# Edge stage of a graph layer: block numbers loaded one or two at a time, accumulator slots cleared by GpSimd, plain addition

## The chip, the cores and the metric

One of the cores of a Trainium2 chip runs the whole program. The metric is device time in microseconds (us) of one execution. Its engines are called as in the profile: PE (TensorE; PEld its weight loads), DVE (VectorE), ACT (ScalarE), POOL (GpSimd) and SP (SyncE); a name with q is an engine's own instruction queue (sequencer).

## What is computed

A node table x of 6250 rows by 256 goes through a layer norm, two graph attention layers plus a linear attention branch, and a mixture of eight experts. The part that matters here is one graph layer; there are two, over the same 106,250 edges, sorted by destination:

```python
q = (x @ Wq + bq).reshape(n, H, C)          # H = 4, C = 64
k = (x @ Wk + bk).reshape(n, H, C)
v = (x @ Wv + bv).reshape(n, H, C)
e = (edge_attr @ We).reshape(-1, H, C)      # edge_attr: 106250 x 194
kj = k[src] + e
vj = v[src] + e
logits = einsum('ehc,ehc->eh', q[dst], kj) / sqrt(C)
ex = exp(logits - segment_max(logits, dst)[dst])
a = ex / (segment_sum(ex, dst)[dst] + 1e-16)
out = segment_sum(vj * a[:, :, None], dst).reshape(n, H * C) + x @ Ws + bs
```

## The kernel before

The nodes form 49 blocks of 128 (NB), the sorted edges tiles of 128. A tile whose edges reach over a block's border is visited once per block, so the work is a list of 880 **slots** (NS), each a pair of a tile and a block. `plan` makes that list on the device: `g.tab` holds, for each slot, the tile's number and, from z.NSP on, the block's number, and `g.flag` is 1 where a slot has the same block as the one before it and 0 where a new block begins.

`nodes` makes the projections of each layer. Keys and values go to memory (`kvD`); the queries of block b stay in SBUF, in the first 256 columns of slot b + 1 of `g.acc`, whose slots have A = 260 columns (four heads of 64 and a denominator each). The edge stage adds up its result in the same array: the sum of block b goes to slot b, which is free once the queries of block b - 1 have been used for the last time. Block b's own queries lie one slot further. The addition L969 has to overwrite the old content at the first slot of a block and to add at the others, so it multiplies what is there by the flag: `acc = acc * flag + pa`.

`edges` (from L745) runs 44 **chunks** of T = 20 slots. Four are written out, then a loop runs 20 times with two chunks a turn (`chunks`, L796), then two more follow in which only late work is left. VectorE, which does a pair of slots at a time (q = 0 to 9 in a chunk), has this order per pair:

- `add` (L964 to L970) of the first slot of a pair that is LAG = 36 slots back;
- L1016, kj: keys plus the edge product; L1028, vj: values plus the edge product;
- `add` of the second slot;
- L1041, the product of kj and the queries; L977, `reduce`, of the pair before.

At fixed q it also does the running maxima over a block: at q = 2 the scans L1061 and L1062 and the copy L1063, at q = 3 the transpose L998, the scans L1024 and L1025 and L1034 to L1036, at q = 4 L1044 and L1056, at q = 5 L1019, L1020 and L1031, at q = 8 the rescaling L1007; at q = 0 and 5 it makes a one-hot matrix (L961, 128 x 1280).

TensorE does, for each slot: two matmuls of the edge attributes (L916; each is two passes in the trace), the queries of the slot's block spread to its edges (L919, two passes) and, for the slot 36 back, the segment sum pa (L938, two passes), which waits for the addition two slots before it. ScalarE makes the weighted values w (L897, L899) and the matrices `oht` (L872, L874). GpSimd issues the gathers of keys and values, one per slot (L859); `kv` is a ring of ten slots, so the two gathers of a pair wait until vj of the pair five earlier is done (L857). SyncE loads the edge attributes, also by a table of numbers.

A block's number picks an address, so it must be in a register of the engine that uses it. `table` (L100) loads a row of numbers from `g.tab` into registers; in the trace this is a TENSOR_LOAD of line L102 in the engine's queue, with the queue's register steps (FUSED_REGOPS, ALU_OP) around it. TensorE loads ten numbers ahead of slots 0 and 10 of a chunk (L912). VectorE loads ten at q = 3 (L1000), ahead of the addition, ten or four at q = 8 (L1002), and six at the head of the loop (L995).

The order of the instructions on each engine is the order of the code; the engines wait for one another by semaphores (`wait_ge`, `need`).

## Time and profile before

| | us |
|---|---|
| median of three runs | 5624.68 |
| lowest and highest run | 5619.65, 5625.87 |
| the profiled execution's own time | 5591.4 |
| its span, first to last instruction | 5589.5 |
| PE busy | 4402.2 |
| DVE busy | 4000.3 |
| ACT busy | 2763.5 |
| POOL busy | 2149.0 |

The two edge stages lie at about 474 to 2403 and 2643 to 4594 us of the span. In the profile a group of instructions is given with its line, engine and operation, what it writes and reads, its count, its busy time and the mean of one, and then the idle time of its engine just before such instructions and what ended it. The releaser "issue" means that the engine waited for nothing that the profile shows, as when its queue is still at work on the instruction.

### The profile page before, as it was taken

To read this page: it belongs to the slowest core of one execution; us is meant where nothing else is said; L and a number is where in the kernel's file an instruction comes from. 1 tells how busy PE (TensorE), PEld (TensorE's weight loads), DVE (VectorE), ACT (ScalarE), POOL (GpSimd) and SP (SyncE) were. 2 spreads that over 40 slices of the span, in tenths; PEclk is the share of its full clock that TensorE was granted. 3 is DMA by queue.
4 is the path that set the end of the run, shared out by engine and by line. 5 is a ranking of instruction groups with operands and counts; after the bars stand their busy time and mean duration, and the time that the engine had idled before them with its cause. 6 is when DMAs were issued, how large, how long until landed. Compare 5 with 4: busy or idle time off the path is not lost. (4 is left out here: it accounts for less than half of the span.)

```text
span 5589.5 us, 99514 instructions
## 1 busy us (share of the span) xinstructions
PE 4402.2 (79%) x18414; PEld 3403.3 (61%) x18415; DVE 4000.3 (72%) x8475; ACT 2763.5 (49%) x10075; POOL 2149.0 (38%) x2298
## 2 busy tenths in 40 slices
PE   3977988888888888878988888888888873139980
PEld 1546777777777777633777777777777752126650
DVE  4446988888888888854988888888888877302222
ACT  0122666666666666631566666666666661013320
POOL 1013544444444444300544444444444424430005
PEclk9999999999999999989999999999999985569995
DMA  4468666666666666534866666666666633432225
GB/s 94 135 217 243 187 182 187 185 181 186 182 191 189 180 187 182 150 112 148 235 185 185 182 181 188 182 183 183 179 186 180 186 102 101 173 97 64 64 78 153
DMA packets 617069, 919.99 MB, mean 165 GB/s; under 512 B 114486, under 2 KB 478582, under 8 KB 616535
## 3 DMA queue, kind: packets, MB, share of 16 engines
q0 software_dynamic: 154544, 502.26, 31.6%
q1 hardware_dynamic: 378966, 326.18, 20.9%
q10 hardware_dynamic: 83280, 89.03, 4.6%
q14 instruction: 251, 2.05, 0.1%
q8 instruction: 28, 0.46, 0.0%
HBM read 803.82 MB, written 113.31 MB: 164 GB/s over the span
## 5 line engine op out<-in xcount | busy, mean ns | idle before, releaser
L859 POOL DMA_INDIRECT edge_kv<-kvD,edge_ix x1760 | 1812.2, 1030 | 1914.7 <-DVE edge_vj L1028 1612.1
L897 ACT ACTIVATE edge_w<-edge_vj,edge_ex 128x64 f32<-128x64 f32 x7040 | 1864.8, 337 | 1012.4 <-PE edge_pa L938 903.6
L916 PE MATMUL edge_ps<-edge_We,edge_ea 112*128 112x256 f32 x7040 | 1906.6, 394 | 201.2 <-issue 173.9
L916 PEld LDWEIGHTS edge_ps<-edge_We,edge_ea 112*128 112x128 f32 x7040 | 1363.4, 196 | 495.5 <-issue 252.8
L938 PE MATMUL edge_pa<-edge_w,edge_oh 128*128 128x260 f32 x3520 | 1143.9, 409 | 309.2 <-DVE acc L969 298.9
L969 DVE SCALAR_TENSOR_TENSOR acc<-acc,flag,edge_pa 128x260 f32 x1760 | 839.2, 477 | 411.8 <-issue 320.7
L919 PE MATMUL edge_ps<-acc,edge_oht 128*128 x3520 | 1089.7, 391 | 0.0
L938 PEld LDWEIGHTS edge_pa<-edge_w,edge_oh 128*128 128x128 f32 x3520 | 647.7, 198 | 523.5 <-issue 322.4
L919 PEld LDWEIGHTS edge_ps<-acc,edge_oht 128*128 128x128 f32 x3520 | 697.8, 198 | 104.5
L1016 DVE TENSOR_TENSOR edge_kj<-edge_kv,edge_ps 128x512 f32<-128x512 f32 x880 | 600.0, 682 | 118.0 <-PE edge_ps L919 114.6
L1041 DVE TENSOR_TENSOR edge_prod<-edge_kj,edge_ps 128x512 f32<-128x512 f32 x880 | 598.6, 680 | 0.0
L1028 DVE TENSOR_TENSOR edge_vj<-edge_kv,edge_ps 128x512 f32<-128x512 f32 x880 | 597.3, 679 | 0.0
L977 DVE TENSOR_REDUCE edge_Lc<-edge_prod 128x8 f32<-128x512 f32 x880 | 597.2, 679 | 0.0
L470 PE MATMUL nodes_pj<-nodes_W,nodes_xT 128*128 128x512 f32 x784 | 361.7, 606 | 28.1 <-ACT nodes_xT L411 28.1
L899 ACT ACTIVATE edge_w<-edge_ex 128x4 f32<-128x4 f32 x1760 | 343.2, 195 | 0.0
L872 ACT ACTIVATE edge_oht<-edge_kb,edge_npart 128x1280 f32<-128x1280 uint8 x178 | 239.9, 1348 | 198.6 <-POOLq L858 101.4
L1544 DVE TENSOR_TENSOR exp_hb<-exp_pH,b 128x512 f32<-128x512 f32 x108 | 74.7, 692 | 325.9 <-PE exp_pH L1487 325.9
L961 DVE TENSOR_TENSOR edge_oh<-free,relS 128x1280 f32<-128x1280 f32 x176 | 260.8, 1482 | 0.0
L470 PEld LDWEIGHTS nodes_pj<-nodes_W,nodes_xT 128*128 128x128 f32 x784 | 144.3, 194 | 182.5 <-issue 146.0
L874 ACT ACTIVATE edge_oht<-edge_oht,ones 128x1280 f32<-128x1280 f32 x178 | 242.5, 1362 | 5.8
L542 DVE TENSOR_TENSOR acc<-nodes_pj,nodes_bias 128x256 f32 (+1 forms) x98 | 41.6, 425 | 236.2 <-PE nodes_pj L470 236.2
L1487 PE MATMUL exp_pH<-W,exp_xT 128*128 x432 | 205.3, 598 | 0.1
(230 smaller groups left out, 2878.6 us busy)
## 6 DMA issues: line engine op xcount, KB each, us to landing
edge_ea<-ea_t_dram SPq DMA_DIRECT2D x1760, 112.0 KB, 3.5
edge_kb<-relD SPq DMA_DIRECT2D x178, 160.0 KB
edge_kv<-kvD,edge_ix POOLq DMA_INDIRECT x1760, 4.4
kvD<-nodes_kvs ACTq DMA_DIRECT2D x98, 256.0 KB
xsD<-mix_zr POOLq DMA_DIRECT2D x27, 512.0 KB
exp_xr<-xsD SPq DMA_DIRECT2D x108, 128.0 KB, 2.1
ysD<-exp_yo ACTq DMA_DIRECT2D x108, 128.0 KB, 1.7
edge_pen<-penD SPq DMA_DIRECT2D x352, 32.0 KB
```

Source lines behind the costliest of these rows:

```text
L470: ins = nc.tensor.matmul(pj[:, j % 2, n * 2 * D:(n + 1) * 2 * D], xT[:, j, c, :], W[:, c, n * 2 * D:(n + 1) * 2 * D], start=(c == 0), stop ...
L859: nc.gpsimd.indirect_dma_start(out=kv[:, j % HT, :], out_offset=None, in_=g.kvD, in_offset=bass.IndirectOffsetOnAxis(ap=ix[:, h, j % HT:j ...
L897: nc.scalar.activation(w[:, j % 4, h * CA:h * CA + C], vj[:, slot, h * C:(h + 1) * C], ACT.Copy, scale=ex[:, x, h, k:k + 1])
L899: nc.scalar.activation(w[:, j % 4, :].rearrange("p (h k) -> p h k", h=H)[:, :, C], ex[:, x, :, k], ACT.Copy).then_inc(s_w, 1)
L916: nc.tensor.matmul(ps[:, j % 4, 0:D], ea[:, j % HT, k, :], We[:, k, :], start=(k == 0), stop=(k == 1))
L919: nc.tensor.matmul(ps[:, j % 4, D:2 * D], oht[:, j // HT, (j % HT) * P:(j % HT + 1) * P], g.q[:, bass.ds(blocks[j % HT], 1), 0:D].rearrang ...
L938: nc.tensor.matmul(pa[:, j % 2, 0:A], oh[:, par, (j + 4) % HT, :], w[:, j % 4, :], start=True, stop=True).then_inc(s_ape, 1)
L969: nc.vector.scalar_tensor_tensor(out=at, in0=at, scalar=g.flag[:, bass.ds(n, 1)], in1=pa[:, j % 2, 0:A], op0=ALU.mult, op1=ALU.add).then_i ...
L977: nc.vector.tensor_reduce(Lc[:, p, :, s:s + 2].rearrange("p h s -> p s h"), prod[:, q % 2, :, :].rearrange("p s (h k) -> p s h k", h=H), A ...
L1016: nc.vector.tensor_tensor(kj[:, q % 2, :, :], kv[:, both, 0:D], e, ALU.add).then_inc(s_kj, 1)
L1028: nc.vector.tensor_tensor(vj[:, p * T + j:p * T + j + 2, :], kv[:, both, D:2 * D], e, ALU.add).then_inc(s_vj, 1)
L1041: nc.vector.tensor_tensor(prod[:, q % 2, :, :], kj[:, q % 2, :, :], ps[:, bank, D:2 * D], ALU.mult).then_inc(s_prod, 1)
```

## The change

- `table` is called for one or two numbers at a time. TensorE loads one number in each slot, between the matmuls of the edge attributes and the one of the queries. VectorE loads two, behind vj, for the pair that follows (`then`, which becomes `here`); only the first pair of a turn of the loop loads its own two at the head.
- `g.acc` has NB + AHEAD slots with AHEAD = 5, and the queries of block b lie in slot b + 5.
- GpSimd clears the slots ahead of the additions. At its start it sets a column `zero` and the slots 0 to 4 of `acc`. Then, once in four slots, it loads one block number, that of the slot 12 back, and copies `zero` over the four slots of `acc` behind that block's (1040 columns), ahead of the gathers of the next two pairs. Each clear counts s_zero up.
- VectorE's addition is `acc = acc + pa`, a tensor_tensor; before the second slot of every other pair it waits for s_zero, for a clear of some five groups earlier.
- `plan` no longer makes `g.flag`, with its broadcast `bb`; the first `nodes` no longer sets parts of `acc` to zero.

```diff
--- before.py
+++ after.py
@@ -36,6 +36,7 @@
 FEW = 255.0
 FAR = 1e30
 T, HT, LAG, RV = 20, 10, 36, 40
+AHEAD = 5
 A = D + H
 CA = C + 1
 
@@ -162,7 +163,6 @@
         kn = st.sb("kn", [P, U * P])
         edge = st.sb("edge", [1, 2])
         wh = st.sb("wh", [P, 2, U])
-        bb = st.sb("bb", [P, NSP], I32)
         r0 = st.sb("r0", [P, NSP])
         pt = st.ps("pt", [P, 2, 4, P])
         s_in, s_iota, s_c = st.sem("s_in"), st.sem("s_iota"), st.sem("s_c")
@@ -181,7 +181,6 @@
                              allow_slow_non_contiguous=True).then_inc(s_tst, 16)
             sp.wait_ge(s_tst, 32)
             sp.dma_start(g.tab[0:1, :], g.tabD.rearrange("r s -> (r s)").unsqueeze(0)).then_inc(s_tld, 16)
-            sp.dma_start(bb[:, :], g.tabD[1, :].partition_broadcast(P)).then_inc(s_bb, 16)
             sp.wait_ge(s_tld, 16)
             sp.wait_ge(s_rel, 1)
             sp.dma_start(g.r0D.rearrange("(j p) -> p j", p=P), rel[:, :, 0], allow_slow_non_contiguous=True).then_inc(s_r0, 16)
@@ -264,9 +263,7 @@
                 link(nc.vector.tensor_scalar(t[:, :], t[:, :], -1.0, FAR, ALU.add, ALU.mult))
                 link(nc.vector.tensor_reduce(wh[:, o, :], t[:, :].rearrange("p (u e) -> p u e", e=P), AX, ALU.min))
             nc.vector.sem_inc(s_w, 1)
-            dve.wait_ge(s_bb, 32)
-            link(nc.vector.tensor_tensor(g.flag[:, 1:NSP], bb[:, 1:NSP], bb[:, 0:NSP - 1], ALU.is_equal))
-            link(nc.vector.memset(g.flag[:, 0:1], 0.0))
+            dve.wait_ge(s_bb, 16)
             link(nc.vector.tensor_scalar(g.oc[:, :], r0[:, 0:z.NS:T], g.part[:, 0:1], C ** -0.5, ALU.is_equal, ALU.mult))
 
         @block.tensor
@@ -475,9 +472,6 @@
         @block.vector
         def _(dve):
             nc.vector.memset(eps[:, :], EPS).then_inc(s_eps, 1)
-            if one:
-                nc.vector.memset(g.acc[:, :, D:A], 0.0)
-                nc.vector.memset(g.acc[:, 0, 0:D], 0.0)
             dve.wait_ge(s_w, 16 * NW)
 
             def statistics(i):
@@ -538,7 +532,7 @@
                 for j in range(UB):
                     b = i * UB + j
                     dve.wait_ge(s_pj, b + 1)
-                    q = g.acc[:, bass.ds(b + 1, 1), 0:D].rearrange("p o d -> p (o d)")
+                    q = g.acc[:, bass.ds(b + AHEAD, 1), 0:D].rearrange("p o d -> p (o d)")
                     nc.vector.tensor_tensor(q, pj[:, j % 2, 0:D], bias[:, 0:D], ALU.add)
                     need(dve, s_st[j], 32 * i)
                     ins = nc.vector.tensor_tensor(kvs[:, j, :], pj[:, j % 2, D:4 * D], bias[:, D:4 * D], ALU.add)
@@ -751,6 +745,7 @@
         ea = st.sb("ea", [EP, HT, 2, P])
         kb = st.sb("kb", [P, 2, HT * P], U8)
         npart = st.sb("npart", [P, 1])
+        zero = st.sb("zero", [P, 1])
         oht = st.sb("oht", [P, 2, HT * P])
         ix = st.sb("ix", [P, 2, HT], I32)
         kv = st.sb("kv", [P, HT, 2 * D])
@@ -785,8 +780,8 @@
         s_kv = [st.sem(f"s_kv{j}") for j in range(HT)]
         s_kb = [st.sem(f"s_kb{h}") for h in range(2)]
         s_pen = [st.sem(f"s_pen{h}") for h in range(2)]
-        s_we, s_np, s_far, s_oht, s_ix, s_step, s_spare, s_pe, s_kj, s_vj, s_prod, s_red = (
-            st.sem(n) for n in ("s_we", "s_np", "s_far", "s_oht", "s_ix", "s_step", "s_spare", "s_pe", "s_kj", "s_vj", "s_prod", "s_red"))
+        s_we, s_np, s_far, s_oht, s_ix, s_step, s_spare, s_zero, s_none, s_pe, s_kj, s_vj, s_prod, s_red = (
+            st.sem(n) for n in ("s_we", "s_np", "s_far", "s_oht", "s_ix", "s_step", "s_spare", "s_zero", "s_none", "s_pe", "s_kj", "s_vj", "s_prod", "s_red"))
         s_oh, s_w, s_ape, s_acc, s_init = (st.sem(n) for n in ("s_oh", "s_w", "s_ape", "s_acc", "s_init"))
         s_resc, s_vinit, s_off, s_abs = (st.sem(n) for n in ("s_resc", "s_vinit", "s_off", "s_abs"))
         s_mt, s_m, s_D, s_et, s_ex, s_Y = (st.sem(n) for n in ("s_mt", "s_m", "s_D", "s_et", "s_ex", "s_Y"))
@@ -844,9 +839,21 @@
 
         @block.gpsimd
         def _(pool):
+            nc.gpsimd.memset(zero[:, :], 0.0).then_inc(s_none, 1)
+            nc.gpsimd.memset(g.acc[:, 0:AHEAD, :], 0.0).then_inc(s_zero, 1)
+            pool.wait_ge(s_none, 1)
+            pool.sem_inc(s_step, 1)
+
             def chunk(c, p, u, kept):
                 for j in range(T):
                     h = j // HT
+                    if j % 4 == 0 and (not isinstance(c, int) or 0 <= c * T + j - 12 < NS):
+                        if not main(c):
+                            pool.wait_ge(s_vj, NS // 2)
+                        pool.wait_ge(s_zero, c * (T // 4) + j // 4 - 2)
+                        block = table(nc, pool, g.tab[0:1, bass.ds(z.NSP + c * T + j - 12, 1)], z.NB - 1)[0]
+                        nc.gpsimd.tensor_copy(g.acc[:, bass.ds(block + 1, AHEAD - 1), :].rearrange("p b n -> p (b n)"),
+                                              zero[:, 0:1].to_broadcast([P, (AHEAD - 1) * A])).then_inc(s_zero, 1)
                     if main(c):
                         if j % HT == 0:
                             need(pool, s_vj, (c - 1) * HT + (h + 1) * (HT // 2))
@@ -908,16 +915,15 @@
                 for j in range(T):
                     s = c * T + j
                     if main(c):
-                        if j % HT == 0:
-                            blocks = table(nc, pe, g.tab[0:1, bass.ds(z.NSP + s, HT)], z.NB - 1)
                         pe.wait_ge(s_ea[j % HT], 32 * c + 16 * (j // HT) + 16)
                         need(pe, s_prod, c * HT + j // 2 - 1)
                         for k in range(2):
                             nc.tensor.matmul(ps[:, j % 4, 0:D], ea[:, j % HT, k, :], We[:, k, :], start=(k == 0), stop=(k == 1))
+                        block = table(nc, pe, g.tab[0:1, bass.ds(z.NSP + s, 1)], z.NB - 1)[0]
                         if j % HT == 0:
                             pe.wait_ge(s_oht, 2 * c + j // HT + 1)
                         nc.tensor.matmul(ps[:, j % 4, D:2 * D], oht[:, j // HT, (j % HT) * P:(j % HT + 1) * P],
-                                         g.q[:, bass.ds(blocks[j % HT], 1), 0:D].rearrange("p o d -> p (o d)"), start=True, stop=True).then_inc(s_pe, 1)
+                                         g.q[:, bass.ds(block, 1), 0:D].rearrange("p o d -> p (o d)"), start=True, stop=True).then_inc(s_pe, 1)
                     if closed(c):
                         if j == 5:
                             pe.wait_ge(s_red, c * HT)
@@ -955,6 +961,7 @@
             for h in range(H):
                 link(nc.vector.tensor_scalar(mask4[:, h:h + 1], g.part[:, :], float(32 * h), None, ALU.is_equal))
             nc.vector.sem_inc(s_init, 1)
+            dve.wait_ge(s_zero, 1)
 
             def onehot(m, par):
                 need(dve, s_ape, HT * m - HT)
@@ -966,8 +973,12 @@
                 dve.wait_ge(s_ape, n + 1)
                 need(dve, s_acc, n)
                 at = g.acc[:, bass.ds(b, 1), :].rearrange("p o n -> p (o n)")
-                nc.vector.scalar_tensor_tensor(out=at, in0=at, scalar=g.flag[:, bass.ds(n, 1)], in1=pa[:, j % 2, 0:A],
-                                               op0=ALU.mult, op1=ALU.add).then_inc(s_acc, 1)
+                if j % 4 == 1:
+                    dve.wait_ge(s_zero, c * (T // 4) + j // 4 - 7)
+                nc.vector.tensor_tensor(at, at, pa[:, j % 2, 0:A], ALU.add).then_inc(s_acc, 1)
+
+            def blocks(n):
+                return table(nc, dve, g.tab[0:1, bass.ds(z.NSP + n, 2)], z.NB - 1)
 
             def reduce(c, p, q):
                 s = 2 * q
@@ -991,15 +1002,11 @@
                     both = slice(j % HT, j % HT + 2)
                     bank = slice(j % 4, j % 4 + 2)
                     e = ps[:, bank, 0:D]
-                    if q == 0 and here is None and lagged(c, 0):
-                        here = [None] * 4 + list(table(nc, dve, g.tab[0:1, bass.ds(z.NSP + c * T - LAG, 6)], z.NB - 1))
+                    if here is None and lagged(c, j):
+                        here = blocks(c * T + j - LAG)
                     if q == 3 and closed(c):
                         step(2)
                         nc.vector.transpose(TT[:, :], FB[:, 112:144]).then_inc(s_m, 1)
-                    if q == 3 and lagged(c, j):
-                        here = table(nc, dve, g.tab[0:1, bass.ds(z.NSP + c * T + j - LAG, HT)], z.NB - 1)
-                    if q == 8 and lagged(c, j):
-                        here = table(nc, dve, g.tab[0:1, bass.ds(z.NSP + c * T + j - LAG, HT if not p and not isinstance(c, int) else 4)], z.NB - 1)
                     if q == 8 and closed(c):
                         dve.wait_ge(s_ex, c)
                         need(dve, s_acc, (c - 1) * T)
@@ -1008,7 +1015,7 @@
                     if lagged(c, j):
                         if q == 8:
                             dve.wait_ge(s_resc, c)
-                        add(c, j, here[(j + 4) % HT])
+                        add(c, j, here[0])
                     if main(c):
                         for k in (j % HT, j % HT + 1):
                             dve.wait_ge(s_kv[k], 32 * c + 16 * (j // HT) + 16)
@@ -1029,13 +1036,20 @@
                     if q == 5 and closed(c):
                         step(12)
                         nc.vector.tensor_scalar(Ym[:, :], mask4[:, :], dl[:, 0:1], None, ALU.mult).then_inc(s_Y, 1)
+                    if q == HT - 1 and (p or isinstance(c, int)):
+                        then = None
+                    elif lagged(c, j + 2):
+                        then = blocks(c * T + j + 2 - LAG)
+                    else:
+                        then = None
                     if q == 3 and closed(c):
                         step(6)
                         nc.vector.tensor_copy(R[:, :], X[:, T:T + 1]).then_inc(s_m, 1)
                         nc.vector.transpose(GX[:, :], X[:, 0:32]).then_inc(s_m, 1)
                         nc.vector.transpose(GY[:, :], Y[:, 1:33]).then_inc(s_m, 1)
                     if lagged(c, j + 1):
-                        add(c, j + 1, here[(j + 5) % HT])
+                        add(c, j + 1, here[1])
+                    here = then
                     if main(c):
                         dve.wait_ge(s_kj, c * HT + q + 1)
                         nc.vector.tensor_tensor(prod[:, q % 2, :, :], kj[:, q % 2, :, :], ps[:, bank, D:2 * D], ALU.mult).then_inc(s_prod, 1)
@@ -1661,11 +1675,10 @@
             g.tab = keep(graph, "tab", [1, 2 * z.NSP], I32)
             g.srcS = keep(graph, "srcS", [P, z.NSP], I32)
             g.relS = keep(graph, "relS", [P, z.NSP])
-            g.flag = keep(graph, "flag", [P, z.NSP])
             g.oc = keep(graph, "oc", [P, z.NS // T])
             plan(nc, z, g, a["src_t"], a["dst_t"], a["dst_first"])
-            g.acc = keep(graph, "acc", [P, z.NB + 1, A])
-            g.q = g.acc[:, 1:z.NB + 1, :]
+            g.acc = keep(graph, "acc", [P, z.NB + AHEAD, A])
+            g.q = g.acc[:, AHEAD:z.NB + AHEAD, :]
             with Stage(nc, "mixkv") as st:
                 g.kTm, g.vm = st.sb("kTm", [P, NP]), st.sb("vm", [P, NP])
                 nodes(nc, z, g, 1, a)
```

The order of the instructions changes at three places. First VectorE in the loop, at q = 3 of the first chunk of a turn. Before:

```order
L998 STREAM_TRANSPOSE edge_TT<-edge_FB 128x32
L102 ISA
L102 TENSOR_LOAD tab
L966 REGISTER_ALU
L969 ISA
L969 SCALAR_TENSOR_TENSOR acc<-acc,flag,edge_pa 128x260
L1015 REGISTER_ALU
L1016 TENSOR_TENSOR edge_kj<-edge_kv,edge_ps 128x512
```

And now:

```order
L1009 STREAM_TRANSPOSE edge_TT<-edge_FB 128x32
L973 REGISTER_ALU
L978 ISA
L978 TENSOR_TENSOR acc<-acc,edge_pa 128x260
L1022 REGISTER_ALU
L1023 TENSOR_TENSOR edge_kj<-edge_kv,edge_ps 128x512
L997 REGISTER_ALU
L1031 SCALAR_TENSOR_TENSOR edge_X<-edge_wp,edge_R,edge_TT 128x20
L1032 SCALAR_TENSOR_TENSOR edge_Y<-edge_wp,edge_TT 128x20
L1035 TENSOR_TENSOR edge_vj<-edge_kv,edge_ps 128x512
L103 ISA
L103 TENSOR_LOAD tab
```

The load between the transpose and the addition is gone; a load of two numbers stands behind vj (L1028 before, L1035 now). The scans L1024 and L1025 read here as SCALAR_TENSOR_TENSOR.

Second TensorE in the loop, around slot 10 of a chunk. Before:

```order
L919 MATMUL edge_ps<-acc,edge_oht 128x256
L935 REGISTER_ALU
L938 MATMUL edge_pa<-edge_w,edge_oh 128x260
L102 ISA
L102 TENSOR_LOAD tab
L913 REGISTER_ALU
L290 REGISTER_ALU
L916 MATMUL edge_ps<-edge_We,edge_ea 128x256 x2
```

And now, in every slot:

```order
L921 MATMUL edge_ps<-edge_We,edge_ea 128x256 x2
L103 ISA
L103 TENSOR_LOAD tab
L925 ISA
L925 MATMUL edge_ps<-acc,edge_oht 128x256
L941 REGISTER_ALU
L944 MATMUL edge_pa<-edge_w,edge_oh 128x260
```

The load has moved from ahead of a half chunk's first matmul to ahead of each slot's query matmul.

Third GpSimd in the loop; the gathers (L859 before) now read L866, and ahead of every fourth of them stand:

```order
L103 ISA
L103 TENSOR_LOAD tab
L855 ISA
L855 COPY acc<-edge_zero 128x1040
L287 REGISTER_ALU
L866 DMA edge_kv<-kvD,edge_ix 128x512 x2
```

Before, only the index copy L853 and its register steps stood between gathers.

## Rows read from the trace of the kernel before

**Rows 1.** The page, part 1: busy us and instructions of each engine

```profile
PE 4402.2 (79%) x18414; PEld 3403.3 (61%) x18415; DVE 4000.3 (72%) x8475; ACT 2763.5 (49%) x10075; POOL 2149.0 (38%) x2298
```

**Rows 2.** By stretch: length; busy of PE, PEld, DVE, ACT, POOL; PEclk; DMA

```profile
710.00:1585.00 875.00, 765.82 (x3285) 627.09 (x3284) 759.84 (x1542) 562.21 (x2121) 422.37 (x441) 0.95 0.65 184
```

**Rows 3.** Costliest groups on VectorE in that stretch: busy, mean ns, idle before, releasers

```profile
L969 DVE SCALAR_TENSOR_TENSOR acc<-acc,flag,edge_pa 128x260 f32 x400 | 190.7, 477 | 93.7 <-issue 72.3 <-PE edge_pa L938 15.4 <-DVE acc L1007 6.0
...
L1016 DVE TENSOR_TENSOR edge_kj<-edge_kv,edge_ps 128x512 f32<-128x512 f32 x200 | 136.3, 682 | 21.4 <-PE edge_ps L919 21.0
```

**Rows 4.** Timeline of VectorE: start us, us, instruction, idle before and releaser

```profile
1513.54 0.21 DVE L998 STREAM_TRANSPOSE edge_TT<-edge_FB 128x32 f32<-128x32 f32 x1
1516.27 0.48 DVE L969 SCALAR_TENSOR_TENSOR acc<-acc,flag,edge_pa 128x260 f32 x1 [2.52 <-issue]
...
1517.27 0.25 DVE L1024 TENSOR_TENSOR_SCAN edge_X<-edge_wp,edge_R,edge_TT 128x20 f32<-128x20 f32 x1
...
1525.09 0.69 DVE L1016 TENSOR_TENSOR edge_kj<-edge_kv,edge_ps 128x512 f32<-128x512 f32 x1 [0.68 <-PE edge_ps L919]
...
1525.89 0.21 DVE L1020 SCALAR_TENSOR_TENSOR edge_dl<-edge_GX,edge_B 128x1 f32<-128x1 f32 x1
```

**Rows 5.** One line's register loads: ns min/median/max, first and last start

```profile
L102 PEldq TENSOR_LOAD <-tab x40: 1077/1747/2429, 730.4 to 1581.2; - x40
...
L102 DVEq TENSOR_LOAD <-tab x1: 2291/2291/2291, 1513.7 to 1513.7; - x1
...
L1471 PEldq TENSOR_LOAD <-etab x216: 297/302/546, 4977.7 to 5420.3; - x108
```

**Rows 6.** Waits of VectorE there: us in total, times, longest us

```profile
DVE acc L969 <- issue: 72.3, 28, 3.0
```

**Rows 7.** Timeline of TensorE: two slots, and the issue wait at a load of ten

```profile
1509.42 1.03 PE L916 MATMUL edge_ps<-edge_We,edge_ea 112*128 112x256 f32 x4
...
1511.16 1.03 PE L916 MATMUL edge_ps<-edge_We,edge_ea 112*128 112x256 f32 x4
...
1521.75 1.13 PE L916 MATMUL edge_ps<-edge_We,edge_ea 112*128 112x256 f32 x4 [1.12 <-issue]
```

**Rows 8.** One line's instructions: queue steps against the engine's own (DVE, then PE)

```profile
L966 DVEq ALU_OP  x1: 40/40/40, 1495.4 to 1495.4; - x1
...
L969 DVE SCALAR_TENSOR_TENSOR acc<-acc,flag,edge_pa x2: 478/479/480, 1495.9 to 1497.5; 128x260 f32 x2
L969 DVEq FUSED_REGOPS  x1: 80/80/80, 1496.5 to 1496.5; - x1
...
L919 PE MATMUL edge_ps<-acc,edge_oht x4: 377/379/381, 1524.5 to 1526.4; 128*128 x4
L919 PEldq FUSED_REGOPS  x1: 55/55/55, 1524.7 to 1524.7; - x1
```

**Rows 9.** Groups by form: VectorE's plain addition from PSUM into acc

```profile
L542 DVE TENSOR_TENSOR acc<-nodes_pj,nodes_bias 128x256 f32 x70 | 29.7, 425 | 162.8 <-PE nodes_pj L470 162.8
```

**Rows 10.** Groups by form on GpSimd

```profile
L859 POOL DMA_INDIRECT edge_kv<-kvD,edge_ix x1760 | 1812.2, 1030 | 1914.7 <-DVE edge_vj L1028 1612.1 <-issue 297.1 <-POOL edge_ix L853 5.5
...
L1155 POOL TENSOR_TENSOR fin_xg<-fin_xn,fin_gam 128x256 f32<-128x256 f32 x49 | 37.0, 760 | 175.6 <-DVE fin_xn L1236 161.7 <-DMA xnD<-fin_xg 13.9
...
L620 POOL MEMSET mix_zr<- 128x1024 f32 x1 | 0.9, 941 | 0.0
```

**Rows 11.** Timeline of GpSimd: the second gathers of two odd pairs

```profile
1513.34 0.95 POOL L859 DMA_INDIRECT edge_kv<-kvD,edge_ix  x1 [0.30 <-issue]
...
1523.67 1.05 POOL L859 DMA_INDIRECT edge_kv<-kvD,edge_ix  x1 [0.31 <-issue]
```

**Rows 12.** Timeline in the finish stage, both engines on SBUF

```profile
4622.30 5.60 DVE L1214 TENSOR_TENSOR fin_x<-acc,fin_rden 128x256 f32<-128x256 f32 x7 [0.23 <-DVE fin_rden L1210]
...
4623.27 0.90 POOL L1158 TENSOR_TENSOR fin_xg<-fin_xg,fin_bet 128x256 f32<-128x256 f32 x1
```

**Rows 13.** Groups by form: the same division where GpSimd is idle

```profile
L511 DVE TENSOR_TENSOR nodes_hs<-acc,nodes_rden 128x256 f32<-128x256 f32 x49 | 20.5, 419 | 1.2 <-DVE nodes_rden L506 1.1
```

## The prediction

> **What bounds the kernel.** The page comes first: no engine is busy for the whole span, TensorE 79%, VectorE 72% [rows 1], and its last chain names only the combine stage. So I cut out ten turns of the edge loop, between 710 and 1585 us [rows 2]: 200 pairs of slots [rows 3], 20 chunks, 87.5 us a turn. VectorE is busy 760 us of the 875 there. What matters is who ends its idle 115 us: 93.7 us lie ahead of its addition L969, 21.4 ahead of its kj L1016 [rows 3]. A layer has 44 chunks, so both layers hold 88, or 44 turns' worth.
>
> The timeline shows what the idle time is. After the transpose L998 at 1513.54 VectorE stands still 2.52 us, "issue" its releaser, until the addition at 1516.27 [rows 4]. In that gap its queue loads ten block numbers: one TENSOR_LOAD, 2291 ns from 1513.7 on [rows 5]. The sequencer can start it only when L998, which waits for VectorE's own scans, has been sent, so nothing covers it. This happens once a chunk. 28 such "issue" waits make 72.3 us of the window [rows 6]: 20 of 2.52 are these; the other 8, 2.7 each, are turns of the loop (two more of the ten turns stand under L938 [rows 3]).
>
> TensorE's queue has loads of the same kind, 1.08 or 2.4 us [rows 5]. Where a slot of TensorE takes 1.74 us, from L916 at 1509.42 to the next at 1511.16, at a load of ten it stands still 1.12 us more, "issue", ahead of 1521.75 [rows 7]. The granted clock is 0.95 of 2.4 GHz over the window [rows 2]. VectorE pays at 1525.09: 0.68 us for L919 [rows 4]. In the window L1016 waits 21.0 us for L919, and 15.4 us of L969's idle time end with L938 [rows 3].
>
> **The change, part by part**, per turn of two chunks.
>
> *VectorE's loads.* Five loads (6, 10, 10, 10 and 4 numbers) become one of two at the head and 19 of two. The trace shows 302 ns for one number, in the expert stage (L1471), and 2291 for ten [rows 5], some 0.22 for each further one, so I take 0.53 us for two, and 0.06 for the address. Each is now sent behind vj. There the sequencer has time: at 1495.4 it had already done the step behind vj (L966) though the addition before, at 1495.9, had not begun, and it did its next, L969's, at 1496.5 [rows 8]. That is 1.0 us of waiting for its own addition, and engine work is queued until 1497.5. So 0.6 to 0.7 us fit, if without much to spare; without that cover each pair would show at most the excess. At q = 3 the load goes behind vj, too, and L998 is followed at once by the addition: of 2 x 2.52 us, 0.1 each stays (the register steps). Gain 4.85; bounds 0 and 5.05. At the loop's head six numbers become two, four fewer at up to 0.22: bounds 0 and 0.9, and I take 0.3. The turn itself, the bulk of 2.7 us, stays.
>
> *TensorE's loads.* One number before each L919, 40 a turn, 0.30 us each plus some 0.1 of register steps. The queue did L919's step at 1524.7 for matmuls of which the last starts at 1526.4 [rows 8], so it is over 1 us ahead; just after a wait the product L938 and the four L916, 1.3 us, cover the load. Cost nothing; if the cover fails, the second rival. The ten-number stops go, and with them VectorE's waits for late products. Those are 21.0 for L1016 plus about 7 of L969's 15.4 (the others are loop heads): 2.8 us a turn. I take 2.5, since a faster VectorE leaves TensorE less room. TensorE needs 3.48 us a pair. VectorE needs 1.00 us from an addition's start past kj to what follows [rows 4], so with 477 and 682 ns as the shares about 0.41 and 0.59, and for a plain pair of two additions and four others 3.2 now and 3.1 then. What is late next is TensorE in plain pairs, made up for where VectorE builds one-hots. Bounds 0 and 2.8, and a little more if the clock stays up.
>
> *The addition.* The scalar_tensor_tensor takes 477 ns on 260 columns [rows 3]. The same engine's plain addition from PSUM into acc takes 425 on 256 [rows 9], so 429 on 260: 0.048 x 40 = 1.9 us, all on VectorE's path. Bounds 0 and 1.9. Its new wait for s_zero is for a clear of 20 slots earlier; behind it are queued that addition and all of VectorE's pair, but the clear is long done.
>
> *GpSimd's clears.* Ten a turn: a load (0.3, under a gather) and a copy of one column onto 1040. No such copy is in the trace. The nearest row is its memset of 128x1024, 941 ns; the other end is its tensor_tensor, 760 ns on 256 [rows 10], which scaled makes 3.1 us. I take 1.06: a memset's rate plus the copy's second operand; one input, one output is nearer to the memset. The engine has room: 40 gathers of 1.03 + 0.30 us [rows 10, 11] are 53, with the ten clears and four index copies 68 of 78. Behind a clear are queued the next index copy, its wait for vj and the gathers; a gather's data are wanted only after four more pairs, some 13 us, against the median 4.4 us to landing, so a delay of 0.5 us is hidden.
>
> But the clear meets VectorE. In the finish stage, while GpSimd runs tensor_tensor, seven L1214, whose inputs both lie in SBUF, take 5.60 us, 0.8 each against GpSimd's 0.90, where the same form L511 takes 0.42 alone [rows 12, 13]. So I count every VectorE instruction of that kind which starts inside a clear as held until its end. (The Trainium skill, SBUF — State Buffer, "Who interferes with whom", calls it an exclusive lock on a shared port pair, held for the whole instruction; the trace agrees, 0.8 against 0.42.)
> When does a clear run? Right behind the second gather of an odd pair. That is 1513.34 + 0.95 = 1514.3, until 1515.35 [rows 11]. Without its stall VectorE comes to the scan L1024 one microsecond after its addition [rows 4], at 1514.75: 0.6 us of wait. The next: gather until 1524.73; L1020, two SBUF inputs, at 1525.89 less the 0.68 that goes, 1525.2, blocked until 1525.8: 0.6 again. The other three clears of a chunk fall among instructions that read PSUM. So +1.2 a chunk, +2.4 a turn; bounds 0 and 4 x 1 for 1.06 us clears.
>
> *The rest.* The plan stage loses the comparison L268 on 895 columns on its last chain, some 1 us at kj's 682 ns for 512 [rows 3]; the broadcast for it lay under longer transfers. The memsets of acc in the first node stage lay under weight loads; two of GpSimd at each edge stage's start lie under VectorE's wait for the first keys. Queries five slots on move an address. Total 1 us.
>
> **Sum.** 4.85 + 0.3 + 2.5 + 1.9 - 2.4 = 7.15 us a turn, times 44 = 315, plus 1: 316. The profiled execution took 5591.4 us (span 5589.5), so it would take 5275. The median of the runs is 33 us above it, 5624.7; I expect that offset to stay: **5309 us**.
>
> **Rivals.** (a) The clears block nobody, the scans being short or the phase another: 9.55 a turn, 5624.7 - 421 = **5204**. Against it the lockstep of the finish stage; for it that the phase is worked out to 0.4 us. 25%.
> (b) Loads show on TensorE's path. If each stops it for 0.4 us, its turn is 40 x (1.74 + 0.4) + 1 = 86.6, and 0.9 x 44 = 40 is all that is left: **5584**. Against it the lead in [rows 8]. 6%.
> (c) A clear costs 2.0 us. The memset makes one access an element at 0.92 ns, the tensor_tensor three at 0.99 each [rows 10]; a copy makes two. Both meetings then last 0.94 longer, 3.8 a turn, 165 in all: **5474**. For it that line through the rows, against it that GpSimd's fixed shares are unknown. 12%. The Trainium skill (GPSIMD Engine Reference, "3.1 Elementwise — side-by-side cycle accounting") puts a tight loop's best case at about 1.8 cycles an element at 1.2 GHz; by that estimate a clear takes 1.6 us and the sum comes to 5401.
> (d) Slower: GpSimd becomes the bound. At tensor_tensor's rate of 3.1 us its turn is 54 + 10 x 3.4 + 2 for its own turn of the loop = 90.0, 2.5 over today's 87.5: gathers land late, VectorE waits at L1016, 5625 + 110 = **5735**. It decides from 2.85 us a clear. Only the two-input row speaks for it. 6%.
> (e) The change does less than it says: the two-number loads overrun their 1.0 us or the semaphore step at q = 3 holds as before, half of 4.85 stays: 5309 + 107 = **5416**. 6%.
> The forecast has 45%.
>
> **How the numbers follow.** The range 5195 to 5480 takes in (a), (c) and (e) and leaves out (b), (d) and tails, under 2 in 10. A measurement of this kernel tells 0.2%, 11 us, from no change. Faster: the forecast, (a), (c), (e) and most of (b), 0.91; slower: (d) and something unseen, 0.06; same 0.03.
>
> **What would show it.** Right: VectorE's "issue" waits ahead of the addition fall from 28 to about 10 in ten turns, the turns of the loop alone; waits of L1016 for L919 nearly gone; the addition near 430 ns; TENSOR_LOAD rows of 0.5 us on VectorE and 0.3 on TensorE; a turn of 80 us; two-SBUF scans of up to 1.2 us where clears run. Wrong if these scans keep their 0.25 us (rival a), if the clear's row reads over 1.5 us (c, d), or if L916 and L938 have "issue" ahead in every slot (b).

## The result and the profile after

| | before | after |
|---|---|---|
| median, us | 5625.27 | 5263.55 |
| lowest and highest run | 5619.65, 5647.71 | 5259.13, 5266.86 |
| the profiled execution's own time | 5591.4 | 5259.1 |
| its span | 5589.5 | 5257.4 |

The ratio is 0.9349, with a 95% interval from 0.9323 to 0.9376: 361.7 us less by the medians, inside the range and 45 us below the forecast of 5309.

The page after, part 1, against [rows 1]:

```profile
PE 4272.0 (81%) x18414; PEld 3307.0 (63%) x18415; DVE 3995.4 (76%) x8471; ACT 2771.4 (53%) x10075; POOL 2655.6 (51%) x2743
```

TensorE is busy 130 us less, VectorE 5 less, GpSimd 507 us more. The same cut as [rows 2], ten turns of the edge loop, is now 793.00 us long instead of 875.00, and the granted clock stays at 1.00 (the level of 2.4 GHz) where it was 0.95:

```profile
699.00:1492.00 793.00, 730.52 (x3282) 601.59 (x3281) 759.33 (x1541) 563.34 (x2123) 536.80 (x541) 1.00 0.71 203
```

The groups of VectorE in that stretch, against [rows 3] and the timeline [rows 4]:

```profile
L978 DVE TENSOR_TENSOR acc<-acc,edge_pa 128x260 f32 x400 | 166.1, 415 | 33.7 <-issue 28.5 <-DVE acc L1014 3.9
...
L1023 DVE TENSOR_TENSOR edge_kj<-edge_kv,edge_ps 128x512 f32<-128x512 f32 x200 | 135.9, 680 | 0.0
...
L1031 DVE TENSOR_TENSOR_SCAN edge_X<-edge_wp,edge_R,edge_TT 128x20 f32<-128x20 f32 x20 | 18.9, 945 | 0.0
L1027 DVE SCALAR_TENSOR_TENSOR edge_dl<-edge_GX,edge_B 128x1 f32<-128x1 f32 x20 | 17.1, 854 | 0.0
```

Three things are to be seen. The addition (L978) has 33.7 us of idle time ahead of it where it had 93.7, and none of it ends with TensorE; kj (L1023) had 21.4, now 0.0. The addition itself takes 415 ns instead of 477. And two small instructions have grown: L1031 (L1024 before), a scan that writes the tile X, from 254 ns to 945, and L1027 (L1020 before) from 210 to 854. The timeline at q = 3 shows what the scan stands in:

```profile
953.23 0.21 DVE L1009 STREAM_TRANSPOSE edge_TT<-edge_FB 128x32 f32<-128x32 f32 x1
...
953.51 0.43 DVE L978 TENSOR_TENSOR acc<-acc,edge_pa 128x260 f32 x1
...
954.05 1.06 POOL L855 COPY acc<-edge_zero 128x1040 f32 x1
...
954.45 0.72 DVE L1031 TENSOR_TENSOR_SCAN edge_X<-edge_wp,edge_R,edge_TT 128x20 f32<-128x20 f32 x1
...
955.09 0.17 DVE L1032 TENSOR_TENSOR_SCAN edge_Y<-edge_wp,edge_TT 128x20 f32<-128x20 f32 x1
```

The addition begins 0.07 us after the transpose's end: the 2.52 us of [rows 4] are gone. GpSimd's clear runs from 954.05 to 955.11. The scan starts at 954.45 and ends at 955.17, right behind the clear, though its work is 0.25 us. At 962.47 L1027 meets the next clear in the same way. The register loads now cost what was taken for them (min, median, max), against [rows 5], and the clear too, against [rows 10]:

```profile
L103 PEldq TENSOR_LOAD <-tab x401: 294/302/322, 698.7 to 1491.6; - x134
...
L103 DVEq TENSOR_LOAD <-tab x200: 523/529/547, 702.4 to 1488.0; - x100
```

```profile
L855 POOL COPY acc<-edge_zero 128x1040 f32 x100 | 106.0, 1060 | 0.4
```

What is left of VectorE's waits, against [rows 6], is the head of each turn, on average 2.44 us, and 0.2 us at four additions of a turn:

```profile
DVE acc L978 <- issue: 28.5, 30, 2.9
DVE acc L978 <- DVE acc L1014: 3.9, 20, 0.2
```

### The profile page after: what moved, and what is told of

The parts are those of the page before. It is cut to its first block and busy times, and to the rows that moved or that the text cites. A ratio compares the mean times of both kernels' runs of the same rounds, so it can differ in the third digit from the quotient of the medians.

```text
span 5257.4 us, 106134 instructions
## 1 busy us (share of the span) xinstructions
PE 4272.0 (81%) x18414; PEld 3307.0 (63%) x18415; DVE 3995.4 (76%) x8471; ACT 2771.4 (53%) x10075; POOL 2655.6 (51%) x2743
## 5 line engine op out<-in xcount | busy, mean ns | idle before, releaser
L866 POOL DMA_INDIRECT edge_kv<-kvD,edge_ix x1760 | 1854.6, 1054 | 1088.6 <-DVE edge_vj L1035 555.8
L921 PE MATMUL edge_ps<-edge_We,edge_ea 112*128 112x256 f32 x7040 | 1835.0, 382 | 30.0 <-DMA edge_ea<-ea_t_dram 17.9
L921 PEld LDWEIGHTS edge_ps<-edge_We,edge_ea 112*128 112x128 f32 x7040 | 1323.6, 190 | 267.2 <-issue 50.7
L944 PE MATMUL edge_pa<-edge_w,edge_oh 128*128 128x260 f32 x3520 | 1099.9, 395 | 247.7 <-DVE acc L978 204.4
L925 PE MATMUL edge_ps<-acc,edge_oht 128*128 x3520 | 1054.8, 380 | 0.3 <-issue 0.3
L944 PEld LDWEIGHTS edge_pa<-edge_w,edge_oh 128*128 128x128 f32 x3520 | 613.9, 189 | 469.5 <-ACT edge_w L906 264.4
L978 DVE TENSOR_TENSOR acc<-acc,edge_pa 128x260 f32 x1760 | 731.0, 415 | 159.8 <-issue 112.0
L925 PEld LDWEIGHTS edge_ps<-acc,edge_oht 128*128 128x128 f32 x3520 | 673.1, 191 | 95.2 <-issue 1.6
L1023 DVE TENSOR_TENSOR edge_kj<-edge_kv,edge_ps 128x512 f32<-128x512 f32 x880 | 598.0, 680 | 37.3 <-issue 17.0
L988 DVE TENSOR_REDUCE edge_Lc<-edge_prod 128x8 f32<-128x512 f32 x880 | 596.3, 678 | 0.0
L1035 DVE TENSOR_TENSOR edge_vj<-edge_kv,edge_ps 128x512 f32<-128x512 f32 x880 | 595.9, 677 | 0.0
L855 POOL COPY acc<-edge_zero 128x1040 f32 x440 | 467.7, 1063 | 36.7 <-DVE edge_vj L1035 32.6
L968 DVE TENSOR_TENSOR edge_oh<-free,relS 128x1280 f32<-128x1280 f32 x176 | 260.8, 1482 | 0.0
```

The costliest lines, as they stand in the source:

```text
L855: nc.gpsimd.tensor_copy(g.acc[:, bass.ds(block + 1, AHEAD - 1), :].rearrange("p b n -> p (b n)"), zero[:, 0:1].to_broadcast([P, (AHEAD - 1 ...
L866: nc.gpsimd.indirect_dma_start(out=kv[:, j % HT, :], out_offset=None, in_=g.kvD, in_offset=bass.IndirectOffsetOnAxis(ap=ix[:, h, j % HT:j ...
L921: nc.tensor.matmul(ps[:, j % 4, 0:D], ea[:, j % HT, k, :], We[:, k, :], start=(k == 0), stop=(k == 1))
L925: nc.tensor.matmul(ps[:, j % 4, D:2 * D], oht[:, j // HT, (j % HT) * P:(j % HT + 1) * P], g.q[:, bass.ds(block, 1), 0:D].rearrange("p o d ...
L944: nc.tensor.matmul(pa[:, j % 2, 0:A], oh[:, par, (j + 4) % HT, :], w[:, j % 4, :], start=True, stop=True).then_inc(s_ape, 1)
L978: nc.vector.tensor_tensor(at, at, pa[:, j % 2, 0:A], ALU.add).then_inc(s_acc, 1)
```

## The experiments

All times are medians. The kernel before took 5629, 5638, 5624 and 5630 us in the four groups in which the kernels ran (e1 to e4, e5 to e8, e9 to e11, e12), so small differences between groups are read from the ratios to the kernel before.

**e1, the clears one pair later.**

```diff
-                    if j % 4 == 0 and (not isinstance(c, int) or 0 <= c * T + j - 12 < NS):
+                    if j % 4 == 2 and (not isinstance(c, int) or 0 <= c * T + j - 14 < NS):
...
-                        block = table(nc, pool, g.tab[0:1, bass.ds(z.NSP + c * T + j - 12, 1)], z.NB - 1)[0]
+                        block = table(nc, pool, g.tab[0:1, bass.ds(z.NSP + c * T + j - 14, 1)], z.NB - 1)[0]
```

> The changed kernel with each of GpSimd's clears one pair later. Theory A (a clear holds every VectorE instruction that reads two SBUF operands and writes SBUF until it ends; in the changed kernel that meets the scan L1031 at q = 3 and L1027 at q = 5, 0.69 + 0.64 us a chunk): one pair later none of the five clears of a chunk lies beside such an instruction, L1031 and L1027 are back at 0.25 and 0.21 us, a turn takes 2.7 us less, 44 turns 117 us: about 5145 us. Theory B (the time lost there is slack that another wait takes up at once, as VectorE waiting for TensorE's L925 ahead of kj): L1023 or L978 show new waits of the same size, 5240 to 5265 us. Theory C (later clears make gathers late): VectorE waits for the gathers ahead of kj, over 5263 us.

5180.89 us, ratio 0.9199 (0.9181 to 0.9218): 83 us less than the change. Groups of VectorE and of GpSimd in ten turns:

```profile
L1023 DVE TENSOR_TENSOR edge_kj<-edge_kv,edge_ps 128x512 f32<-128x512 f32 x199 | 134.9, 678 | 1.7 <-DMA resD<-mix_xo 1.7
...
L1031 DVE TENSOR_TENSOR_SCAN edge_X<-edge_wp,edge_R,edge_TT 128x20 f32<-128x20 f32 x20 | 5.1, 254 | 0.0
...
L1027 DVE SCALAR_TENSOR_TENSOR edge_dl<-edge_GX,edge_B 128x1 f32<-128x1 f32 x20 | 4.1, 206 | 0.0
```

```profile
L855 POOL COPY acc<-edge_zero 128x1040 f32 x100 | 106.0, 1060 | 0.5
```

The same hundred clears of the same 1060 ns run, and the two instructions are back at 254 and 206 ns. So it was the place of the clears that made them long, and little took up what was freed (theory B falls). A turn falls from 79.3 to 77.05 us, 2.3 and not 2.7, and the time by 83 us and not by theory A's 117. A few other instructions are met instead (over both layers 4 of L1070 with 995 ns, 470 alone, and 2 of L1038 with 1728, 225 alone), and while VectorE's busy time falls by 106 us, its idle time in the edge stages grows by 22.

**e2, the old form of the addition with the clears.**

```diff
-                nc.vector.tensor_tensor(at, at, pa[:, j % 2, 0:A], ALU.add).then_inc(s_acc, 1)
+                nc.vector.scalar_tensor_tensor(out=at, in0=at, scalar=g.ones[:, 0:1], in1=pa[:, j % 2, 0:A],
+                                               op0=ALU.mult, op1=ALU.add).then_inc(s_acc, 1)
```

> The changed kernel with the addition as scalar_tensor_tensor again, but times a fixed column of ones (so the clears stay). Theory A (the form of the instruction makes the 62 ns between 477 and 415): the addition reads 477 ns, 1760 of them cost 0.062 x 1760 = 109 us: 5370 us. Theory B (part of the 477 ns came from the flag's address in a register or from its reading beside other work): the addition reads about 430 ns, 5290 us. The prediction's own price, 0.048 us each, would be 5347 us.

5340.52 us, 77 more than the change. The addition takes 473 ns with a fixed scalar too:

```profile
L978 DVE SCALAR_TENSOR_TENSOR acc<-acc,ones,edge_pa 128x260 f32 x400 | 189.3, 473 | 34.4 <-issue 29.2 <-DVE acc L1015 3.9
...
L1028 DVE SCALAR_TENSOR_TENSOR edge_dl<-edge_GX,edge_B 128x1 f32<-128x1 f32 x20 | 15.6, 781 | 0.0
L1032 DVE TENSOR_TENSOR_SCAN edge_X<-edge_wp,edge_R,edge_TT 128x20 f32<-128x20 f32 x20 | 12.2, 608 | 0.0
```

The form makes the 58 ns, 0.058 x 1760 = 102 us, and theory B falls. It gives only 77, in the main because the slower VectorE comes to the clears later: L1032 (the scan of X here) takes 608 ns, not 945, and L1028 781, not 854, together 0.41 us a chunk, 36 us for 88 at the rate of these ten turns.

**e3, the loads alone; e4, TensorE's; e5, VectorE's.** All three start from the kernel before; flag and multiplication stay. e4 has the first of these edits, e5 the second, e3 both:

```diff
-                        if j % HT == 0:
-                            blocks = table(nc, pe, g.tab[0:1, bass.ds(z.NSP + s, HT)], z.NB - 1)
...
+                        block = table(nc, pe, g.tab[0:1, bass.ds(z.NSP + s, 1)], z.NB - 1)[0]
```

```diff
-                    if q == 3 and lagged(c, j):
-                        here = table(nc, dve, g.tab[0:1, bass.ds(z.NSP + c * T + j - LAG, HT)], z.NB - 1)
...
+                    elif lagged(c, j + 2):
+                        then = blocks(c * T + j + 2 - LAG)
```

> The kernel before with only the loads changed (TensorE one number a slot, VectorE two behind vj); flag, scalar_tensor_tensor and the queries' places as before, no clears. Theory A (VectorE's load stalls 4.9, loop head 0.6, TensorE's late products 2.8 us a turn, as the trace of the changed kernel suggests): 8.3 x 44 = 365 us off 5625: 5260 us, the same as the whole change, because the clears' 2.7 and the addition's 2.5 us a turn cancel. The prediction's own terms (4.85 + 0.3 + 2.5): 5288 us. Theory B (clears and plain addition bring more than they cost): 5300 us or more.

> The kernel before with only TensorE's loads changed (one number in each slot); VectorE still loads ten. Theory A (the 2.8 us a turn that VectorE waited for late L919 and L938 is all of TensorE's part): 123 us off: 5500 us, L1016's waits for L919 gone, the 2.52 us stalls still there. Theory B (TensorE makes its late slots good while VectorE stands in its own loads, so that most is hidden): 5560 to 5625 us. Theory C (forty single loads show on TensorE): over 5625 us.

> The kernel before with only VectorE's loads changed (two numbers behind vj); TensorE still loads ten ahead of each half chunk. With TensorE's loads alone the time fell 133 us, with both 337. Theory A (the two sets of stalls add up): 337 - 133 = 204 us off 5629: 5425 us. Theory B (while VectorE stands in its own loads TensorE catches up, so without them TensorE's stops show in full): L1014 (kj) waits more for L919 than the 21 us in ten turns of before, less is gained: 5450 to 5500 us. Price by the trace of before alone, (4.9 + 0.6) x 44 = 242 us: 5387 us.

| | us | ratio (95%) | off |
|---|---|---|---|
| e4, TensorE's | 5496.35 | 0.9766 (0.9745 to 0.9787) | 133 |
| e5, VectorE's | 5489.20 | 0.9744 (0.9724 to 0.9764) | 148 |
| e3, both | 5291.55 | 0.9398 (0.9381 to 0.9415) | 337 |

The parts don't add up: 281 alone, 337 together. The waits of VectorE in ten turns of e4 and then of e5 tell why:

```profile
DVE acc L968 <- issue: 79.3, 37, 3.1
...
DVE edge_kj L1015 <- PE edge_ps L918: 3.2, 4, 2.1
```

```profile
DVE acc L969 <- PE edge_pa L938: 30.8, 26, 2.3
DVE edge_kj L1015 <- PE edge_ps L919: 25.7, 24, 2.2
DVE acc L969 <- issue: 17.4, 22, 2.8
```

In e4 the waits for TensorE are nearly gone and VectorE's own 2.52 us stops are there as before. In e5 it is the other way round: 17.4 us of "issue" instead of 72.3, but 56.5 us of waiting for L938 and L919, where the kernel before had 15.4 + 21.0. So while VectorE stood in its load of ten, TensorE made up for its own; without that rest its stops show in full (theory B). The granted clock goes with these stops of TensorE and of the engine it waits for: 0.95 in ten turns before, 0.97 in e4 and in e5, 1.00 (2.4 GHz throughout) in e3. So part of the 56 us that the two parts lack may be the clock's; no run tells it apart.

**e6, four chunks in a turn of the loop, clears as in e1.**

```diff
-            with eng.Fori(2, NCH // 2) as i:
-                kept = chunk(2 * i, 0, i, None)
-                chunk(2 * i + 1, 1, i, kept)
+            with eng.Fori(1, NCH // 4) as i:
+                kept = None
+                for k in range(4):
+                    kept = chunk(4 * i + k, k % 2, 2 * i + k // 2, kept, k < 3)
...
-                    if q == HT - 1 and (p or isinstance(c, int)):
+                    if q == HT - 1 and not more:
```

> The kernel with the clears one pair later (5181 us), and four chunks in a turn of the loop instead of two: 10 turns a layer instead of 20. In that kernel VectorE stands 2.5 us ahead of the first addition of each turn. Theory A (this is the price of the turn itself, branch and load of the first two numbers, and nothing covers it): 10 turns x 2 layers x 2.5 = 50 us less: 5131 us. Theory B (the longer body costs as much in other ways, as instructions that come late, or it only moves the stall into the body): 5175 to 5190 us.

5226.97 us: 46 more than e1, not 50 less. The first layer's edge stage takes the same as in e1 (1730 us), the second 1778 instead of 1730. The waits of VectorE in the turns of the first layer, and of the second:

```profile
DVE acc L979 <- PE edge_pa L945: 33.3, 10, 4.5
```

```profile
DVE acc L979 <- PE edge_pa L945: 72.7, 10, 9.1
```

Ten waits in ten turns, 3.3 us each, and 7.3 in the second layer, and now for TensorE's L945. TensorE's timeline at the head of such a turn, and the code queues in one turn of e6 and in one of e1:

```profile
3073.73 0.69 PE L922 MATMUL edge_ps<-edge_We,edge_ea 112*128 112x256 f32 x2 [4.10 <-issue]
3077.86 1.01 PE L922 MATMUL edge_ps<-edge_We,edge_ea 112*128 112x256 f32 x2 [3.43 <-issue]
3078.67 1.13 PE L926 MATMUL edge_ps<-acc,edge_oht 128*128 x2
```

```profile
q8 instruction: 11, 0.18, 0.5%
q14 instruction: 22, 0.18, 0.4%
```

```profile
q14 instruction: 5, 0.04, 0.1%
```

TensorE stands for 4.10 and again for 3.43 us with nothing to wait for that the profile shows, and the queues that carry instructions (q8, q14) move 33 packets in the turn, where a turn of two chunks has 5, none on q8. At the head of e1's turns TensorE's timeline has no such stop; there it is VectorE that stands 2.5 us of "issue". I read this as the longer body being fetched anew in every turn; no row ties a packet to a stop. (The Trainium skill, Runtime: NRT & Kernel Launch, "Instruction fetch mechanics", says that a taken branch out of the part of the program which an engine holds makes it wait for a fetch; the trace fits that, 7.5 us of "issue" and the 33 packets.) Why the second layer pays twice as much stays open.

**e7, each clear as four copies of 260 columns.**

```diff
-                        nc.gpsimd.tensor_copy(g.acc[:, bass.ds(block + 1, AHEAD - 1), :].rearrange("p b n -> p (b n)"),
-                                              zero[:, 0:1].to_broadcast([P, (AHEAD - 1) * A])).then_inc(s_zero, 1)
+                        for k in range(AHEAD - 1):
+                            nc.gpsimd.tensor_copy(g.acc[:, bass.ds(block + 1 + k, 1), :].rearrange("p b n -> p (b n)"),
+                                                  zero[:, 0:1].to_broadcast([P, A])).then_inc(s_zero if k == AHEAD - 2 else s_spare2, 1)
```

> The changed kernel, clears where they are, each written as four copies of 260 columns instead of one of 1040. Theory A (what a VectorE instruction with two SBUF operands waits for is the end of the one GpSimd instruction that it meets): a hold lasts at most about 0.3 us, L1031 and L1027 read some 0.4 and 0.35 us instead of 0.95 and 0.85, about 1.1 us a chunk less, up to 97 us: 5170 to 5190 us, if a copy of 260 takes near 0.3 us. Theory B (GpSimd keeps the port from copy to copy, or VectorE loses each new race for it): L1031 and L1027 stay over 0.8 us: 5263 us. Theory C (a fixed share in each copy makes the four much longer than 1.06 us together): the meetings shift, and GpSimd's time per clear over 2 us delays gathers: 5263 us or more.

5246.09 us, 17 less than the change. Groups of VectorE, then of GpSimd:

```profile
L979 DVE TENSOR_TENSOR acc<-acc,edge_pa 128x260 f32 x401 | 166.7, 416 | 41.8 <-issue 36.0 <-DVE acc L1015 3.9
...
L1033 DVE TENSOR_TENSOR_SCAN edge_Y<-edge_wp,edge_TT 128x20 f32<-128x20 f32 x20 | 6.3, 315 | 0.0
...
L1032 DVE TENSOR_TENSOR_SCAN edge_X<-edge_wp,edge_R,edge_TT 128x20 f32<-128x20 f32 x20 | 5.3, 267 | 0.0
...
L1028 DVE SCALAR_TENSOR_TENSOR edge_dl<-edge_GX,edge_B 128x1 f32<-128x1 f32 x20 | 4.3, 217 | 0.0
```

```profile
L856 POOL COPY acc<-edge_zero 128x260 f32 x403 | 145.2, 402 | 0.5
```

L1032 and L1028 read 267 and 217 ns, and this is no shift past the clears: 78 of the 88 L1028 of both layers run beside two copies of a clear and take 208 ns all the same, and no L1032 takes over 556. L1033 takes 315 ns, for 174 in the change when no clear is beside it, so some of the hold is left. VectorE gets in between two copies: what holds it is one GpSimd instruction, not the row of them. VectorE's busy time falls by 87 us. But its idle time grows by 63: the head of a turn takes 3.2 us instead of 2.4, and kj at q = 3 stands 0.6 more. Four copies also keep GpSimd busy for 1.45 us a clear, not 1.06. Why the head grew wasn't tried apart.

**e8, two more copies ahead of each clear, clears as in e1.**

```diff
+                        need(pool, s_spare2, 2 * (c * (T // 4) + j // 4 - 3))
+                        pool.sem_inc(s_step, 1)
+                        for k in range(2):
+                            nc.gpsimd.tensor_copy(junk[:, k, :], zero[:, 0:1].to_broadcast([P, (AHEAD - 1) * A])).then_inc(s_spare2, 1)
```

> The kernel with the clears one pair later (5181 us), with two more copies of the same size to a spare tile ahead of each clear: 3.2 us of copying a clear instead of 1.06. It tests the price of the rival in which GpSimd becomes the bound. Theory A (GpSimd's time adds up and it has 24 us of waiting for vj and its own index copies to give in ten turns, its other idle time is the issue of gathers): a turn of GpSimd is 41.6 of gathers + 11.6 issue + 31.8 of copies + 1 + 2 = 88 us, VectorE's 77 is under it: 11 us a turn more, 44 turns 484: about 5665 us, VectorE waiting ahead of kj for gathers. Theory B (the issue time between gathers shrinks when more lies in the queue, or VectorE's meetings with the copies are the greater loss): 5300 to 5550 us, with two-SBUF scans of 1 to 3 us.

5624.69 us, the time of before (ratio 0.9982, 0.9963 to 1.0001), near theory A's 5665, but VectorE loses the time in another way. VectorE's and GpSimd's groups:

```profile
L1028 DVE TENSOR_TENSOR edge_kj<-edge_kv,edge_ps 128x512 f32<-128x512 f32 x199 | 135.3, 680 | 17.1 <-PE edge_ps L930 10.4 <-DMA edge_kv<-kvD,edge_ix 4.1 <-issue 2.5
...
L973 DVE TENSOR_TENSOR edge_oh<-free,relS 128x1280 f32<-128x1280 f32 x40 | 94.6, 2364 | 0.0
L1075 DVE TENSOR_TENSOR_SCAN edge_B<-edge_pen,edge_GY,edge_F 128x128 f32<-128x128 f32 x20 | 43.8, 2191 | 0.0
```

```profile
L871 POOL DMA_INDIRECT edge_kv<-kvD,edge_ix x403 | 400.1, 993 | 141.0 <-issue 95.4 <-POOL edge_ix L865 31.2 <-DVE edge_vj L1040 7.8
```

GpSimd is full, as theory A has it: only 7.8 us of its idle time end with vj, where it had 136 in the change, and a turn takes 87.1 us for the 88 that theory A gave GpSimd's own work. But VectorE waits for gathered data only 4.1 us in ten turns, where theory A expected its loss. The loss stands in its own instructions: B (the scan L1075) 2191 ns instead of 470, the one-hots (L973) 2364 instead of 1482, in both edge stages 3619 us busy instead of 3241 in e1. Copies of 3.1 us a clear cost the whole gain of the change and of e1 together. How much of that the holds would cost by themselves e8 doesn't show, since GpSimd's own work fills the turn as well.

**e9, no clears.** From the change, without the clear and the addition's wait for it; the sums then start from whatever the slot held, so the clearing of `acc` is left out of the computation. The memset of the denominators' columns in the first `nodes` is back.

```diff
-                        nc.gpsimd.tensor_copy(g.acc[:, bass.ds(block + 1, AHEAD - 1), :].rearrange("p b n -> p (b n)"),
-                                              zero[:, 0:1].to_broadcast([P, (AHEAD - 1) * A])).then_inc(s_zero, 1)
...
-                if j % 4 == 1:
-                    dve.wait_ge(s_zero, c * (T // 4) + j // 4 - 7)
```

> The changed kernel without GpSimd's clears and without the additions' wait for them (the sums start from what was in the slot). With the clears one pair later the kernel took 5181 us, where they lie now 5263. Theory A (where they lie now the clears cost VectorE what L1031 and L1027 read more, 1.29 us a chunk over both layers, and nothing else): 5263 - 113 = 5150 us, 30 us less than with the later clears, which then still cost some gathers that come late. Theory B (the later clears cost nothing): 5175 to 5185 us. Theory C (GpSimd's time weighs by itself, through the gathers): under 5140 us.

5169.47 us, 94 less than the change, 11 less than e1. So the clears cost 2.1 us a turn at the change's place. One pair later they cost at most 0.3, and that isn't clear of noise: the ratios are 0.9191 (0.9173 to 0.9209) here and 0.9199 (0.9181 to 0.9218) in e1.

**e10, four numbers a load on VectorE; e11, on TensorE too; both from e1.**

```diff
             def blocks(n):
-                return table(nc, dve, g.tab[0:1, bass.ds(z.NSP + n, 2)], z.NB - 1)
+                return table(nc, dve, g.tab[0:1, bass.ds(z.NSP + n, 4)], z.NB - 1)
...
+                    elif j % 4 == 0:
+                        then = here
...
-                        block = table(nc, pe, g.tab[0:1, bass.ds(z.NSP + s, 1)], z.NB - 1)[0]
+                        if j % 4 == 0:
+                            fours = table(nc, pe, g.tab[0:1, bass.ds(z.NSP + s, 4)], z.NB - 1)
+                        block = fours[j % 4]
```

> The kernel with the clears one pair later (5181 us), VectorE loading four numbers for two pairs in place of two for one. In the kernel before, TENSOR_LOADs of four numbers whose place in the table is a multiple of four took 0.35 us, ten at other places 2.29. Theory A (such a group of four loads as one): a load reads 0.35 us instead of 0.53, half as often; the queue's stops of 0.2 us at the pairs q = 5 and at the loop's head shrink, 0.2 to 0.5 us a turn: 5160 to 5175 us. Theory B (the loads are hidden already): 5175 to 5185 us. Theory C (four numbers cost 0.3 + 3 x 0.22 = 1.0 us, just the sequencer's slack): stops in every other pair, over 5190 us.

> The kernel with the clears one pair later (5181 us), with four numbers a load on VectorE and on TensorE too. Theory A (TensorE's single loads are hidden, so that only the shorter code counts; VectorE as in the run with four numbers on it alone): within 10 us of that run, 5160 to 5175 us. Theory B (part of the 2.4 us ahead of a turn's first addition is code that TensorE's queue fetches, 30 register loads and their steps a turn less shorten it): a loop head of under 2.2 us, 5150 to 5165 us.

e10 takes 5138.64 us, e11 5132.59. The loads of e11:

```profile
L103 PEldq TENSOR_LOAD <-tab x101: 327/332/348, 706.0 to 1469.5; - x101
L103 DVEq TENSOR_LOAD <-tab x101: 340/344/366, 707.8 to 1471.4; - x101
```

Four numbers come in 344 ns where two took 529: theory A, and its size was set too low, 42 us and not 5 to 20. VectorE's idle time in the two edge stages falls by 33 us: the stops at q = 5 are gone (0.22 and 0.23 us a turn) and the head falls from 2.49 to 2.34, 24 us of the 33 in 40 turns. The other 9 of the 42 us aren't assigned; by the ratios, 0.9134 and 0.9199, e10 and e1 are 37 us apart. e11's 6 us are below what can be told.

**e12, e11 with no loop.**

```diff
-            for c in range(4):
-                chunk(c, c % 2, c // 2, None)
-            with eng.Fori(2, NCH // 2) as i:
-                kept = chunk(2 * i, 0, i, None)
-                chunk(2 * i + 1, 1, i, kept)
-            for c in range(NCH, NCH + after):
-                chunk(c, c % 2, c // 2, None)
+            kept = None
+            for c in range(NCH + after):
+                kept = chunk(c, c % 2, c // 2, kept)
```

> The kernel with clears one pair later and four numbers a load on both engines (5133 us), with all 44 chunks of a layer written out, so that no engine jumps back. With four chunks a turn the edge stage of the second layer took 47 us longer, its VectorE standing 6.6 to 9.1 us at each jump back, and the code queues moved 20 + 9 packets a turn where two chunks a turn needed 5. Theory A (those stops are code that has to be fetched after a jump back; code in sequence is fetched in time): no stop at the head of a pair of chunks, 2.2 us x 40 = 88 us less: 5045 us. Theory B (the stop is only the branch and its registers, and the 47 us had another cause): also near 5045 us, but with the code queues' packets few. Theory C (more code to fetch, and fetches queue behind the gathers and the edge attributes): waits of one to several us for issue spread over the stages, 5133 us or more.

5035.80 us, ratio 0.8948 (0.8933 to 0.8963): 97 less than e11, and the best version here, 228 us under the change. The window, the waits of VectorE and the code queues in 800 us of it:

```profile
700.00:1500.00 800.00, 777.96 (x3554) 653.79 (x3553) 793.99 (x1672) 605.70 (x2300) 569.85 (x586) 1.00 0.77 219
```

```profile
DVE edge_kj L1021 <- PE edge_ps L923: 4.1, 3, 1.8
...
DVE acc L976 <- issue: 0.3, 1, 0.3
```

```profile
q8 instruction: 33, 0.54, 0.3%
q14 instruction: 63, 0.52, 0.2%
```

VectorE works 794 of 800 us. 96 code packets came, some 9 in the time of two chunks where e11 has 5, and nothing waited for them. So the stop of 2.2 us belongs to the head of a turn, not to the amount of code. The head is the jump back and the turn's first load of numbers, which here lies behind vj like the others; the load alone takes 0.34 us (e11), and the two weren't tried apart.

## Why the prediction was right, and what was mis-sized

The forecast's case was the one that came: loads no longer stop the queues, the addition is shorter, and two clears a chunk hold VectorE. Its sum against the runs, each in us of the whole time (44 turns):

| term | predicted | measured |
|---|---|---|
| loads of both engines and the head | 4.85 + 0.3 + 2.5, 337 | 337 (e3) |
| addition without flag | 1.9, 84 | 122 (e3 to e9; 116 by the ratios) |
| clears meeting VectorE | -2.4, -106 | -94 (e9 to the change; -89 by the ratios) |

**VectorE's loads.** Right: in the change 0.06 us are left of each 2.52, a load of two is 529 ns, hidden behind vj. The queue's slack was close, as said: where a long pair's instructions are short (q = 5), 0.23 us show. **TensorE's loads.** Right: 302 ns each, and no waits for L919 left. What the prediction didn't see is that the two gains lean on each other, e4 and e5; its terms were read from one trace in which both stops stood, and hold only for both together. **The loop's head** gave 0.6 us for 0.3: 0.2 in the first layer, and 1.0 in the second, where the head took 3.5 us before and which the prediction's ten turns don't cover. That the loads' sum came out to the microsecond is in part luck. In the loops of e3 VectorE's stops at q = 3 give 4.9 us a turn, the head 0.8 and TensorE's late products 2.8, 8.5 together, and stops of its own queue that the kernel before didn't show, most of them at q = 5, take 0.9 back.

**The addition** was the mis-sized term: "0.048 x 40 = 1.9 us". The instruction takes 415 ns, not 429; the row of 425 ns [rows 9] was one of another shape and place. A turn of e3, which keeps the flag, is 2.8 us longer than one of e9. The addition itself is 474 ns there, 59 more, which makes 2.4 us; the other 0.5 is idle time of VectorE. Its small stops ahead of the addition are 0.48 and 0.44 us at two places of a turn (q = 8 of the first chunk, q = 5 of the second) where the change, e9 and e2 have 0.20 and 0.23. e2 has the same form of addition as e3 but a fixed scalar, so these stops go with the flag's column, whose address comes from a register. The queue's step of the addition in e3 and in e2:

```profile
L968 DVEq FUSED_REGOPS  x400: 53/80/86, 709.8 to 1502.6; - x134
```

```profile
L978 DVEq FUSED_REGOPS  x380: 57/57/64, 714.3 to 1518.1; - x190
```

The prediction counted the multiplication's time and not the register step for the flag's column.

**The clears.** The mechanism, the place and the price held: 1.06 us a clear, predicted 1.06 (between rows that allowed 0.94 to 3.1, so the exact hit is luck); holds of 0.69 and 0.64 us at L1031 and L1027, predicted 0.6 each. Rival (a), that they block nobody, falls by e1 and the timeline; clears that meet hardly anything gave 5181 where it had 5204. Rivals (c) and (d) fall by the clear's row. As to (d), e8 shows that its price was near (a turn of 87.1 us with copies of 3.1 us, where (d) had 90.0) and GpSimd full, but that VectorE's loss doesn't show as waits for gathers: it is held by the copies instead. Rivals (b) and (e) fall by the waits.

**The sum.** By the profiled executions 332 us came off, 316 predicted: a loop turn gave 8.14 us, not 7.15, but only 40 of the 44 turns' worth lie in the loops, and the chunks written out gave 10 us instead of 29. By the medians 362 came off. The step "I expect that offset to stay" failed: the profiled execution of before lay 33 us under its median, the one of the change 4. That makes 29 of the 45 us by which the forecast was too high; the other 16 are the sum's.

**What would show it** came as written, with "issue" waits of 30 for about 10 as the exception: 10 of them are the heads, the others 0.2 us each.

## What to carry to other kernels

Before an engine gets new work on SBUF, list which of its neighbour's instructions run beside it and read two SBUF operands; moving the new work by one step of the order can save what a cheaper instruction can't. Take stops of two engines away together or expect less, for each hides in the other's. And where an engine stands at the head of every turn of a loop, try both directions of its length: a longer body cost 46 us here, no loop at all gave 97.

## What the runs showed of the hardware

- VectorE and GpSimd: a VectorE instruction with two SBUF operands, however short, that starts while GpSimd copies SBUF ends right behind the copy (of the change's scans L1031, 254 ns alone, the 42 that started inside a clear took 706 ns on average and ended 61 to 68 ns behind it). One whose recorded start lies just ahead of the copy's is held as well (38 scans up to 56 ns ahead, 1169 ns on average). Additions and products with one operand in PSUM keep their time beside the same copy (418 against 415 ns). Gathers issued by GpSimd don't hold VectorE (the scan of B takes 473 ns beside them in e9). A reduction of one SBUF operand (L988) isn't held either, 680 ns.
- Register loads: one number 302 ns, two 529, ten whose place isn't a multiple of four 2291, but four whose place is one 344 on VectorE and 332 on TensorE, and ten from such a place 1061 (VectorE, before). This fits a price per separate read, with an aligned group of four as one read.
- The head of a turn costs with the length of the body: VectorE stands 2.2 to 2.5 us with two chunks, its first load included, and 3.3 and 7.3 on average in the two layers with four, at most 9.1 (some 1820 instructions of TensorE a turn instead of 910), with 29 to 33 code packets a turn instead of 5. A straight program of 44 chunks showed no such wait.
